# A 96-column product for own keys and first level, and unread products in two waits of the first round (RWKV and state-space block, one core)

## The reference

```python
def step(S, inp):
    r_t, k_t, v_t, d_t = inp
    kv = k_t[..., :, None] * v_t[..., None, :]
    y = jnp.einsum('bhj,bhji->bhi', r_t, S + u[None, :, :, None] * kv)
    return (d_t[..., None] * S + kv, y)
...
xn = _layernorm(x, axis=-1)
s = _L0_attn_ref(xn, ...)
g = _silu(_L0_ffn_ref(xn, ...))
x = x + s * g
xn = _layernorm(x, axis=-1)
s = _L1_attn_ref(xn, ...)
g = _silu(_L1_ffn_ref(xn, ...))
x = x + s * g
```

## Time and profile before

| what | us |
|---|---|
| median of 3 runs | 759.26 |
| lowest and highest | 757.93, 760.34 |
| the profiled execution, its own time | 756.95 |
| its span, first to last instruction | 755.2 |
| PE busy | 725.2 (96%) |
| ACT busy | 315.2 (42%) |
| DVE busy | 527.1 (70%) |
| mean granted clock of PE | 0.993 |

### The profile page before, as it was taken

How to read it: one execution, slowest core, us unless ns; L and a number is a source line. 1 busy time by engine, 2 the same in 40 slices (tenths; PEclk the granted TensorE clock), 3 DMA queues, 4 the chain that set the end, 5 groups by cost and what they waited for, 6 DMA issues and landing times.

```text
span 755.2 us, 18230 instructions
## 1 busy us (share of the span) xinstructions
PE 725.2 (96%) x7136; PEld 591.8 (78%) x7136; DVE 527.1 (70%) x1200; ACT 315.2 (42%) x644; POOL 75.7 (10%) x85
## 2 busy tenths in 40 slices
PE   5896999999999999999999999999999999999897
PEld 3675678887788788887888868888788878788676
DVE  2896679856798378965789467974679737896243
ACT  1321594216732367114752058321673236711670
POOL 6201011001011010100110001100101101010020
PEclk9998999999999999999999999999999999999999
DMA  8810252015500354003630145101531035300460
GB/s 282 348 30 14 78 108 45 1 45 155 90 10 1 86 142 71 3 14 101 127 57 2 30 141 95 34 1 48 162 65 26 0 84 141 72 3 13 115 111 15
DMA packets 121601, 56.01 MB, mean 74 GB/s; under 512 B 104304, under 2 KB 113584, under 8 KB 119856
## 3 DMA queue, kind: packets, MB, share of 16 engines
q1 hardware_dynamic: 121520, 54.76, 29.6%
HBM read 42.35 MB, written 12.40 MB: 72 GB/s over the span
## 4 chain that ended last, share of the span: by engine, by line
PE 92%; DVE 5%; issue 1%; ACT 0%; DMA 0%; POOL 0%; SPq 0%; DVEq 0%; ACTq 0%; POOLq 0%
PE psum L1361 71%; PE psum L1463 4%; PE psum L1573 2%; PE psum L1558 2%; PE psum L1434 1%; PE psum L1611 1%; PE psum L1584 1%; PE psum L1773 1%; PE psum L1409 1%; PE psum L1389 1%; PE psum L1446 1%; PE psum L1423 1%; PE psum L1722 1%; PE psum L1617 1%; PE psum L1483 1%
## 5 line engine op out<-in xcount | busy, mean ns | idle before, releaser
L581 ACT ACTIVATE BC<-psum 64x256 f32<-64x256 f32 x128 | 81.1, 634 | 3.5 <-PE psum L1361 1.8
L1361 PE MATMUL psum<-xnT,sb_f_gate 128*128 128x256 f32 x248 | 62.3, 394 | 0.8 <-ACT xnT L594 0.8
L1361 PE MATMUL psum<-xn1T,sb_n_gate 128*128 128x256 f32 x256 | 61.4, 383 | 0.0
L1361 PE MATMUL psum<-xn1T,sb_n_up 128*128 128x256 f32 x256 | 60.5, 379 | 0.0
L1361 PE MATMUL psum<-xnT,sb_f_up 128*128 128x256 f32 x240 | 59.0, 388 | 0.0
L1361 PEld LDWEIGHTS psum<-xn1T,sb_n_up 128*128 128x128 f32 x256 | 48.6, 190 | 6.6
L1361 PEld LDWEIGHTS psum<-xnT,sb_f_gate 128*128 128x128 f32 x248 | 46.7, 194 | 8.5 <-ACT xnT L594 1.2
L1361 PEld LDWEIGHTS psum<-xn1T,sb_n_gate 128*128 128x128 f32 x256 | 47.4, 190 | 6.5
L1361 PEld LDWEIGHTS psum<-xnT,sb_f_up 128*128 128x128 f32 x240 | 43.6, 189 | 7.6 <-DVE S L1058 1.7
L1361 PE MATMUL psum<-sb_f_down,hid 128*128 128x256 f32 x224 | 49.5, 379 | 0.0
L1361 PE MATMUL psum<-sb_n_down,hidB 128*128 128x256 f32 x224 | 49.5, 379 | 0.0
(11 more groups left out here) (212 smaller groups left out, 1511.4 us busy)
## 6 DMA issues: line engine op xcount, KB each, us to landing
cs_row<-cs_dram SPq DMA_DIRECT2D x8, 1024.0 KB, 4.8
x_dram<-gate SPq DMA_DIRECT2D x8, 512.0 KB, 2.8
cs_half<-cs_dram SPq DMA_DIRECT2D x16, 256.0 KB, 5.7
hidB<-x_dram SPq DMA_DIRECT2D x8, 512.0 KB, 5.8
b_dram<-B_turned SPq DMA_DIRECT2D x32, 128.0 KB, 3.4
hidB<-b_dram SPq DMA_DIRECT2D x8, 512.0 KB, 4.4
X<-in_x SPq DMA_DIRECT2D x9, 256.0 KB, 3.1
XT<-in_x_turned SPq DMA_DIRECT2D x8, 256.0 KB, 2.9
```

Source lines behind the costliest of these rows:

```text
L581: ins = a_.activation(cols[:, par, 2 * pair:2 * pair + 2, :], src[64 * par:64 * par + 64, :, s, :], ACT.Identity)
L1361: ins = t_.matmul(ps(t, name)[first_row:first_row + rows, col:col + n], w, x, start=(k == 0), stop=(k == len(ws) - 1))
```

## The change

1. `rU` grows from 64 to 96 columns for each block of 64 tokens: 64 with the bonus and, behind them, the 32 odd tokens' receptances without it. ACT writes these with an added activation ahead of the two of the bonus.
2. `own_products` multiplies with all 96 columns; `level_first` is gone. The products of level 0 now lie in D0 and D1, and L0 and L1 are opened at level 1.
3. DVE starts level 0 when D0 and D1 are filled, lets PE go on to level 1 behind the two scalings (not behind the copy), and copies level 0 and own keys from the blocks of 96.
4. In the first round `kept_at_work` puts products ahead of the two waits, identity times a part of `f_down`, into banks that are written anew afterwards: 7 calls and 6 calls. Nothing reads them.

```diff
-        rU = sb("rU", [P, CH, T])
+        rU = sb("rU", [P, CH * NQ * 2, 96])
...
                     wait_filled(act, a, "r")
+                    by_64 = ps(a, "r")[:, :].rearrange("p (b x) -> p b x", x=64)
                     a_.activation(flat(rT), ps(a, "r")[:, :], ACT.Identity)
+                    a_.activation(rU[:, :, 64:96], by_64[:, :, 1:64:2], ACT.Identity)
...
-                        ins = a_.activation(rU[:, h, :], ps(a, "r")[:, h * T:(h + 1) * T], ACT.Identity,
+                        ins = a_.activation(rU[:, 4 * h:4 * h + 4, 0:64], by_64[:, 4 * h:4 * h + 4, :], ACT.Identity,
                                             scale=vec[:, u0:u0 + 1])
...
+            def level_take_0(t):
+                odd = own[:, :, :, :].rearrange("p e g (b two) -> p e g b two", two=2)[:, :, :, :, 1]
+                data = by_half(t, "D")[:, :, 0:384].rearrange("p e (g x) -> p e g x", x=96)[:, :, :, 64:96]
+                return d.copy_predicated(odd, masks[:, 0, :].rearrange("p (e g b) -> p e g b", e=2, b=32), data)
...
-                dve.wait_ge(lev_done, t.count(6, n + 1))
-                for ins in level_update(t, LEVELS[n]):
-                    did(ins)
+                if n == 0:
+                    for e in range(2):
+                        wait_filled(dve, t, f"D{e}")
+                        dve.sem_inc(passed, 1)
+                else:
+                    dve.wait_ge(lev_done, t.count(5, n))
+                k_ins, q_ins = level_update(t, LEVELS[n])
+                did(k_ins)
+                if n == 0:
+
+                    q_ins.then_inc(lev_ready, 1)
+                    did(level_take_0(t))
+                    return
+                did(q_ins)
...
             def own_keys(t):
 
-                dve.wait_ge(lev_ready, t.count(6, 1))
-                dve.sem_inc(passed, 1)
+                after()
...
-            def level_first(t):
-
-                open_bank(t, "L0")
-                open_bank(t, "L1")
-                pe.sem_inc(passed, 1)
-                level_products(1).then_inc(lev_done, 1)
...
-                        ins[e] = t_.matmul(by_half(t, "D")[64 * hf:64 * hf + 64, e, g * 64:(g + 1) * 64], flat(kT)[r, n:n + 64],
-                                           flat(rU)[r, n:n + 64], start=True, stop=True)
+                        ins[e] = t_.matmul(by_half(t, "D")[64 * hf:64 * hf + 64, e, g * 96:(g + 1) * 96], flat(kT)[r, n:n + 64],
+                                           rU[r, 2 * g + hf, :], start=True, stop=True)
...
                 pe.wait_ge(lev_ready, t.count(6, n))
                 pe.sem_inc(passed, 1)
+                if n == 1:
+                    open_bank(t, "L0")
+                    open_bank(t, "L1")
+                    pe.sem_inc(passed, 1)
...
+                def kept_at_work(name, count):
+
+
+                    open_bank(a, name)
+                    for _ in range(count):
+                        t_.matmul(ps(a, name)[:, 0:C], ident[:, :], W["f_down"][:, 0:C], start=True, stop=True)
...
                     down_part(a, 1, 0, 4)
+                    kept_at_work("yT", 7)
                     pe.wait_ge(sparse_ready, a.count(2, 2))
...
                     next_up_0()
+                    kept_at_work("xT1", 6)
                     turned_1()
```

More of the change, by code:

```diff
@@ L948, in own_keys @@
             def own_keys(t):
-                dve.wait_ge(lev_ready, t.count(6, 1))
-                dve.sem_inc(passed, 1)
+                after()
                 for e in range(2):
-                    wait_filled(dve, t, f"D{e}")
-                    dve.sem_inc(passed, 1)
-                    free(d.copy_predicated(own[:, e, :, :].rearrange("p g x -> p (g x)"), same[:, 256 * e:256 * e + 256],
-                                           by_half(t, "D")[:, e, 0:256]), t, f"D{e}")
+                    data = by_half(t, "D")[:, e, 0:384].rearrange("p (g x) -> p g x", x=96)[:, :, 0:64]
+                    free(d.copy_predicated(own[:, e, :, :], same[:, 256 * e:256 * e + 256].rearrange(
+                        "p (g x) -> p g x", x=64), data), t, f"D{e}")
             def last_update(t):
@@ L1700, in first_levels @@
                     own_products(a)
-                    level_first(a)
                 def keys_turned():
```

## The result

| | median us | runs | lowest, highest |
|---|---|---|---|
| before | 758.83 | 5 | 756.66, 760.34 |
| after | 750.66 | 5 | 749.61, 750.87 |

The ratio is 0.9885, 95% interval 0.9863 to 0.9907: 8.2 us faster by the medians, where 3.7 were forecast and the range ended at 753.4. The profiled execution of after took 750.87 us, with a span of 749.1, against 756.95 and 755.2.

The account below looks back on a forecast made before the run. PE was taken to bound the kernel (92% of the chain), its stages summing to the time in the seven rounds. Terms -2.2 - 1.5 - 0.2 + 0.2 = -3.7 us gave 755.6 us, range 753.4 to 759.0.

Parts of the forecast that it names:

- The two waits: First round, PE waiting 3.78 and 3.20 us: unread products keep the clock up, gaining 2.2 and 1.5 us.
- The stage of 96 columns: Own keys and level 0 on PE in one stage: 0.82 us, 0.25 us less in each of seven rounds.
- the activation: Added ACT activation ahead of own keys delays PE: 0.28 us more in each round.
- Rivals C: 96-column stage: four quadrants no longer run side by side, 759.6 us two at a time, 768.6 one; chance 0.07.
- D: 96-column stage costs what 64 columns do, 0.24 us more gained a round, 753.9 us; chance 0.12.
- E: Added ACT activation costs 0.64 us because its words lie apart, 758.1 us; chance 0.09.
- The rule on PSUM lines: ACT's added read: skill wants consecutive elements adjacent in two-value PSUM lines, this uses every second; no price given.
- The first round: PE waits there for the second bank of own keys: 0.2 us gained, between nothing and 0.4.
- the net of the rounds: Seven rounds of both layers: 0.28 lost minus 0.25 gained, 0.03 us a round, 0.2 us lost in all.
- the chance of 0.05 for slower: Whole kernel measurably slower: most of the case where 96-column quadrants stop running side by side.
- The base: Profiled execution 756.95 us, median 759.26, difference unexplained by the clock; the same 3.7 us gain put on the median.

Follow-up runs that it names:

- same_places: Change without unread products, plus PE increments, 64 ahead of the loop and 64 in each later round, restoring old instruction places: 756.58 us, ratio 0.9967.
- before_pad52: Kernel before plus 52 PE semaphore increments ahead of the seven-round loop, nothing else: 778.22 us, ratio 1.0257.
- the version of 747.96 us: Changed kernel with the gate mix moved behind the receptances' product in the seven rounds of both layers: 747.96 us, ratio 0.9863.
- before_again: Kernel before, unchanged, run again to see every run's clock: 758.25 us over 12 runs, ratio 1.0004.
- front_warm: The version of 747.96 us plus 8 unread products of 256 columns ahead of PE's wait for the first norm: 760.15 us, ratio 1.0011.

## Why the prediction was wrong, step by step

- **The two waits** (2.2 and 1.5): right, in the trace (2.24 and 1.57), in the runs (3.9, where 3.7 were forecast), and in their mechanism: waits of 0.76 and 0.61 us, clock 1.00, then POOL's root as the next bound (DVE waits 1.03 us for it, and PE 0.39 for DVE ahead of L1440).
- **The stage of 96 columns** (0.82) and **the activation** (0.28 on the path): right, 0.82 and 0.27. Rivals C, D and E are out. The rule on PSUM lines that I set against the change ("Advanced Engine Details and Errata", Memory Cachelines, of the Trainium skill) has no effect that this trace shows: reading each second word took 0.378 us, and the activation of the same size with adjacent words 384 ns.
- **The first round** (0.2 for DVE's levels): the stretch gave 0.9 us up to the up product behind the gate's mix, because the stop of 0.86 us there went, which the forecast took for fixed. What is left for DVE's levels is too little to be told.
- **The step that failed** is the sentence "In the seven rounds of both layers PE has no wait worth naming; there the sum of its stages is the time", and with it the net of the rounds, 0.2 us lost. The stages are not only work. In before some contain stops that have no releaser, and I carried them over unchanged. The change takes 64 instructions out of each round and puts 52 ahead of the loop, and the boundaries of PE's blocks fall elsewhere: 2.3 us less in five of the rounds and 0.9 in the first. That the stops go with the place is shown: they stand at record 1338 and at record 450 in the kernels with the old places, the increments in the old places (same_places) brought the first kind back, and those in the kernel before (before_pad52) moved the second to another call. Of the wide product's 4.8 us same_places gives 2.3 to 3.4 to places; the rest is open.
- **A term that the sum did not have** is the ninth round. PE waits 1.55 us in before for the load of `hidB`, and not at all in after, in the profiled executions. This is no boundary. PE's idle time there differs by 0.5 us between two executions of the same kernel, and nothing here shows that the change earned the 1.6 us. A way from the places to that load exists, but is only argued. Over all rounds of all 15 traces the load took 4.0 to 4.4 us wherever no packet of the instruction queue fell into it, and 4.1 to 5.9 where one did; in the ninth round only the three traces with the old places in the loop have such a packet, and their loads took 4.7, 5.1 and 5.4 us, the others 4.1 to 4.4.
- That the time fell beyond the forecast, and did not rise, was luck. The same 52 instructions without the wide product cost 14.6 us, and 32 more on the version of 747.96 us cost 12. The range had no room for either; the chance of 0.05 for slower did not rest on this.
- **The base**: the same 3.7 us were put on the median. The profiled execution of before lay 1.9 us below its median, that of after 0.2 above. The prediction said that the clock does not explain this difference; before_again speaks against that, since the executions with the lowest mean clock were the longest. The executions of after lie within 1.3 us, those of before within 3.7.

The Trainium skill has the mechanism: "Runtime: NRT & Kernel Launch", Instruction fetch mechanics, has blocks of 16 KiB or 256 instructions, fetched in sequence, and says that a taken branch to a page that is not there stalls. The size agrees with these traces (stops at records 1338, 38 and 6 behind the loop's start and at record 450, all on one raster of 256). The same section calls the crossing of a boundary "mostly hidden". Here it was hidden beside long records, cost 0.13 to 0.69 us in the stage of 64-column records and 0.86 to 1.63 at record 450. Short records alone do not decide it: in after record 450 lies in a level product of 32 columns, and PE does not stop there.

## What to carry to other kernels

If the trace has idle time of the engine on the critical path with "issue" as its reason, find out first which kind it is. If it ends a fixed 0.1 us behind the end of another engine's instruction in every trace, it is a wait; the ninth round was one. If it moves to another call when instructions are added ahead of it, and keeps its record number, it is a block boundary. Then count how many instructions the edit adds or removes ahead of it and where the boundaries of 256 fall afterwards. A boundary 6 or 38 records behind a loop's start cost 1.4 to 2.7 us in each iteration that a taken branch leads to, one at 54, 58, 70 or 78 little or nothing at the start of the loop; a few idle instructions ahead of the loop, where the engine waits anyway, move it. And if a version is slower than its parts explain, try 16 of them before you drop the idea.

## What the runs showed that I had not expected

- An increment of a semaphore on PE takes 0.15 us from one to the next, and 64 of them beside records of 0.216 us in each round cost nothing that the times show (749.76 against 750.66 us).
- At the start of before, PE's records of 256 columns take about 0.45 us from one to the next, twice the later 0.216, while the row of windows for 7 to 13 us has the granted clock at 1.00. With unread products ahead they take 0.23. This slow start does not show in the granted clock, and what it is stays open.
- The clock does not fall at once behind every stop, and does not go by the length of one stop alone. Of the five in the kernel with the unread products alone, the records right behind those of 2.72, 2.17 and 1.86 us were slow. Behind the other 2.72 and the 1.90 the steps' product still ran at the short pace, and the clock fell within 2 us of the restart:

```profile
359.00:361.00 2.00, 2.00 (x7) 0.38 (x9) 0.00 (x0) 0.15 (x2) 0.00 (x0) 0.50 0.20 25
...
449.60:451.60 2.00, 2.00 (x19) 1.10 (x19) 0.00 (x0) 1.07 (x4) 0.00 (x0) 0.68 0.62 222
```

  But with increments in the kernel before (before_pad52) it stayed at 1.00 behind stops of 2.61, 2.45 and 2.53 us, with unread products at the start (front_warm) behind all five in the loop, and rests of 2.25 us behind transposes left it up.
